# Routing's one-hot matrices with the tile index innermost in pairs, made and multiplied in two halves

## The reference

```
logits = xf @ router_w.T + router_b            # layer 0: 32 experts, the best one
idx = argmax(logits); h = relu(x @ W1[idx] + b1[idx]); out = relu(h @ W2[idx] + b2[idx])
probs = softmax(xf @ gate_w + gate_b)          # layer 1: 8 experts, the best two, weighted
out = sum over the best two of weight * (gelu(x @ W1[e] + b1[e]) @ W2[e] + b2[e])
values, idx = top_k(x @ Wg + bg + bias, 2)     # layer 2: 8 experts, the best two
out = sum over the best two of softmax(values) * (relu(x @ W1[e] + b1[e]) @ W2[e] + b2[e])
```

## Time and profile before

| | us |
|---|---|
| median of three runs | 2290.98 |
| profiled execution, its own time | 2291.57 |
| its span in the profile | 2289.7 |
| TensorE busy | 1947.9 (85%) |
| VectorE busy | 1574.2 (69%) |
| ScalarE busy | 1111.3 (49%) |
| GpSimd busy | 443.3 (19%) |

### The profile page before, as it was taken

One profiled execution on the slowest core, in us unless ns is written; L12 is line 12 of the kernel. 1 busy time (PEld: TensorE's weight loads), 2 busy tenths in 40 slices (PEclk: granted clock), 3 DMA queues, 4 the chain that ended last, 5 costly groups with the idle time before them and its releaser, 6 DMA issues.

```text
span 2289.7 us, 42272 instructions
## 1 busy us (share of the span) xinstructions
PE 1947.9 (85%) x15872; PEld 1314.7 (57%) x15872; DVE 1574.2 (69%) x3183; ACT 1111.3 (49%) x2198; POOL 443.3 (19%) x455
## 2 busy tenths in 40 slices
PE   6999296899999999749966698669967999999788
PEld 3877263688888887637744577557754222222343
DVE  6866665655555577746667888645567999999555
ACT  7555275523223244427745677346545223232654
POOL 0000474100000022137741000057620000000000
PEclk9999697999999999969987899879988999999899
DMA  6999367556566589556754567433332343232000
GB/s 197 315 343 328 122 151 163 210 199 246 219 230 243 220 324 404 191 191 218 231 165 133 148 168 179 164 98 93 85 110 73 115 122 90 82 90 85 0 21 29
DMA packets 236971, 389.10 MB, mean 170 GB/s; under 512 B 20640, under 2 KB 189216, under 8 KB 221025
## 3 DMA queue, kind: packets, MB, share of 16 engines
q1 hardware_dynamic: 211972, 333.86, 44.4%
q0 software_dynamic: 15296, 43.88, 7.3%
q10 hardware_dynamic: 9504, 8.65, 1.2%
HBM read 304.55 MB, written 81.78 MB: 169 GB/s over the span
## 4 chain that ended last, share of the span: by engine, by line
PE 51%; DVE 27%; ACT 8%; DMA 8%; issue 4%; POOL 2%; SPq 1%; ACTq 0%; DVEq 0%; POOLq 0%
DVE BIG L2819 7%; PE ps L1078 6%; PE ps L1080 6%; PE ps L1079 6%; PE ps L283 5%; PE ps L284 4%; PE ps L285 4%; PE ps L2320 4%; PE ps L2641 4%; DMA BIG<-in_adjT 3%; PE ps L2647 2%; PE ps L2322 2%; DMA X<-rows_split,idxg 2%; DVE BIG L1735 2%; DVE BIG L1743 2%
## 5 line engine op out<-in xcount | busy, mean ns | idle before, releaser
L1078 PE MATMUL ps<-R,BIG 128*128 128x256 f16 (+1 forms) x1764 | 486.1, 276 | 13.4 <-DVE BIG L1110 8.6
L1080 PE MATMUL ps<-R,BIG 128*128 128x256 f16 (+1 forms) x1764 | 483.5, 274 | 0.0
L1079 PE MATMUL ps<-R,BIG 128*128 128x256 f16 x1764 | 483.4, 274 | 0.0
L2641 PE MATMUL ps<-BIG 128*64 128x452 f32 x1056 | 230.9, 558 | 23.9 <-DVE BIG L2819 20.1
L1078 PEld LDWEIGHTS ps<-R,BIG 128*128 128x128 f16 x1764 | 171.9, 97 | 41.3 <-DVE BIG L1110 9.1
L2819 DVE SCALAR_TENSOR_TENSOR BIG<-BIG 128x904 f32<-128x904 f32 x176 | 192.4, 1155 | 1.6
L1079 PEld LDWEIGHTS ps<-R,BIG 128*128 128x128 f16 x1764 | 173.8, 98 | 21.5
L1080 PEld LDWEIGHTS ps<-R,BIG 128*128 128x128 f16 x1764 | 172.0, 98 | 24.5
L2703 ACT ACTIVATE BIG<-X,BIG 128x64 f32<-128x64 f32 x264 | 70.2, 337 | 232.8 <-PE ps L2647 232.7
L2641 PEld LDWEIGHTS ps<-BIG 128*64 128x64 f32 x1056 | 64.4, 136 | 186.4 <-issue 131.1
L2320 PE MATMUL ps<-BIG,X 128*128 x464 | 155.6, 382 | 9.6 <-DVE X L2379 9.6
(11 more groups left out here) (419 smaller groups left out, 4489.8 us busy)
## 6 DMA issues: line engine op xcount, KB each, us to landing
BIG<-adj_split SPq DMA_DIRECT2D x63, 1376.0 KB, 6.5
BIG<-in_adjT SPq DMA_DIRECT2D x42, 1408.0 KB, 10.8
BIG<-in_adj SPq DMA_DIRECT2D x22, 1408.0 KB, 9.2
BIG<-in_adjT SPq DMA_DIRECT2D x66, 452.0 KB, 3.3
adj_split<-BIG SPq DMA_DIRECT2D x21, 1376.0 KB, 10.9
XX<-in_f SPq DMA_DIRECT2D x70, 256.0 KB, 7.9
experts_split<-XX SPq DMA_DIRECT2D x64, 256.0 KB, 4.4
BIG<-experts_split SPq DMA_DIRECT2D x16, 1024.0 KB, 13.0
```

Source lines behind the costliest of these rows:

```text
L1078: pe.matmul(out[:, 0:n], pr[:, 0, k, :], h[:, k, 0:n], start=start, stop=False)
L1079: pe.matmul(out[:, 0:D], pr[:, 0, k, :], l[:, k, 0:D], start=False, stop=False)
L1080: return pe.matmul(out[:, 0:n], pr[:, 1, k, :], h[:, k, 0:n], start=False, stop=stop)
L2641: pe.matmul(ps[rs, 2 * (h // 2) + c, 0:CW], self.G[:, u, h * HF:(h + 1) * HF], self.PT[:, u, h, cs], start=start, stop=stop)
```

## The change

Four things change. The one-hots are laid out with the tiles of rows in pairs innermost: element (pair of tiles, lane or list tile, which of the two). The numbers 0 to 127 and 0 to J-1, each doubled, come from two small tables that GpSimd writes into X2 (`lanes`, `tiles`; semaphore `tb`) in each of the three layers. VectorE makes the one-hots choice by choice, in A parts (one in layer 0, two in layers 1 and 2), and raises `oh` after each; TensorE multiplies each part as it is ready and reads R and T with a step of two elements. ScalarE loads Gelu's table at the end of layer 1's routing. In the experts of layers 1 and 2 TensorE does hidden(0) ahead of turn(1).

```diff
-                s.wait(pe, "oh", 1)
                 J = self.J
-                n = self.A * KT
-                R, T = self.R(), self.T()
-                for q in range(n):
-                    mm = pe.matmul(ps[:, 0, 0:2 * J], R[:, q, :], T[:, q, :], start=q == 0, stop=q == n - 1)
+                for a in range(self.A):
+                    s.wait(pe, "oh", a + 1)
+                    R, T = self.R(a), self.T(a)
+                    for q in range(KT):
+                        mm = pe.matmul(ps[:, 0, 0:2 * J], R[:, q // 2, :, q % 2], T[:, q // 2, :, q % 2], start=a + q == 0,
+                                       stop=a == self.A - 1 and q == KT - 1)
                 mm.then_inc(s["lm"], 1)
...
+            def pairs(space, at, n, count=PR):
+                return space[:, at:at + n * count].bitcast(F16).rearrange("p (q c r) -> p q c r", q=count, r=2)
+
+            def R(self, a):
+                return self.pairs(XX, a * P * PR, P)
+
+            def T1(self, a):
+                return self.pairs(XX, P * KT + a * self.J * PR, self.J)
+
+            def T(self, a):
+                return self.pairs(X2, P * KT + a * self.J * KT, 2 * self.J)
+
+            def lanes(self):
+                return self.pairs(X2, 0, P, 1)
+
+            def tiles(self):
+                return self.pairs(X2, P, self.J, 1)
+
+            def tables(self, pool, *free):
+                for z, n in free:
+                    pool.wait_ge(z, n)
+                for out, row16, n in ((self.lanes(), lane16, P), (self.tiles(), tile16, self.J)):
+                    pool.tensor_copy(out, row16[:, 0:n].rearrange("p (q c o) -> p q c o", q=1, o=1).to_broadcast([P, 1, n, 2]))\
+                        .then_inc(self.st["tb"], 1)
...
                 W[self.i + 1].act(act)
+                if self.kind == "softmax":
+                    act.preload_act_table_set("gelu_and_others")
...
-                v.tensor_tensor(T1, tile16[:, 0:J].rearrange("p (o j) -> p o j", o=1).to_broadcast([P, q, J]),
-                                high.rearrange("p (q o) -> p q o", o=1).to_broadcast([P, q, J]), ALU.is_equal)
-                link(v.tensor_tensor(R, lane16[:, :].rearrange("p (o c) -> p o c", o=1).to_broadcast([P, q, P]),
-                                     low.rearrange("p (q o) -> p q o", o=1).to_broadcast([P, q, P]), ALU.is_equal))
-                v.tensor_scalar(T2[:, :, 0:J], T1, pos1[:, 0:1], None, ALU.mult)
-                v.tensor_tensor(T2[:, :, J:2 * J], T1, which[:, 0:q].rearrange("p (q o) -> p q o", o=1).to_broadcast([P, q, J]),
-                                ALU.mult).then_inc(s["oh"], 1)
+                s.wait(v, "tb", 2)
+                for a in range(A):
+                    T1, T2 = self.T1(a), self.T(a)
+
+                    def tile_row(z, n):
+                        return z[:, a * KT:(a + 1) * KT].rearrange("p (q o r) -> p q o r", o=1, r=2).to_broadcast([P, PR, n, 2])
+
+                    v.tensor_tensor(T1, self.tiles().to_broadcast([P, PR, J, 2]), tile_row(high, J), ALU.is_equal)
+                    link(v.tensor_tensor(self.R(a), self.lanes().to_broadcast([P, PR, P, 2]), tile_row(low, P), ALU.is_equal))
+                    v.tensor_scalar(T2[:, :, 0:J, :], T1, pos1[:, 0:1], None, ALU.mult)
+                    v.tensor_tensor(T2[:, :, J:2 * J, :], T1, tile_row(which, J), ALU.mult).then_inc(s["oh"], 1)
...
                 turn(0)
+                hidden(0)
                 turn(1)
-                hidden(0)
...
             p0.pool(pool)
+            r0.tables(pool, LC.done[1], s0.st.end("tx"))
             r0.pool(pool)
...
             p1.pool(pool)
+            r1.tables(pool, (p1.st["ag"], p1.st.at("ag") + 2 * KT + KT))
             many_rows.pool(pool)
...
             c1.pool(pool)
+            r2.tables(pool, *e1.done, *top.done)
             p2.pool(pool)
```

More of the change, by code:

```diff
@@ L1779, in __init__ @@
                 self.J, self.G, self.size = TILES[E], GROUPS[E], GROUP[E]
-                self.st = Stage("route", lm=1, v=0, a={"argmax": 0, "softmax": 2, "top2": 2}[kind], mk=1, rk=2, oh=1, ix=1,
-                                cw=1, sel=16 if i == 0 else 16 * 9)
+                self.st = Stage("route", lm=1, v=0, a={"argmax": 0, "softmax": 2, "top2": 2}[kind], mk=1, rk=2, oh=self.A, ix=1,
+                                cw=1, tb=2, sel=16 if i == 0 else 16 * 9)
                 self.done = [self.st.end("cw"), self.st.end("sel")]
@@ L1824, in pe @@
                 mm.then_inc(s["rk"], 1)
-                s.wait(pe, "oh", 1)
                 J = self.J
-                n = self.A * KT
-                R, T = self.R(), self.T()
-                for q in range(n):
-                    mm = pe.matmul(ps[:, 0, 0:2 * J], R[:, q, :], T[:, q, :], start=q == 0, stop=q == n - 1)
-                mm.then_inc(s["lm"], 1)
[L1833 to L1841, removed]
+                for a in range(self.A):
[4 more added lines that the diff above has]
+                                       stop=a == self.A - 1 and q == KT - 1)
+                mm.then_inc(s["lm"], 1)
+            @staticmethod
+            def pairs(space, at, n, count=PR):
[16 more added lines that the diff above has]
+                        .then_inc(self.st["tb"], 1)
             def act(self, act):
@@ L1953, in dve @@
                 link(v.tensor_copy(low, posu[:, 0:A, :].rearrange("p a t -> p (a t)")))
-                q = A * KT
-                R, T1, T2 = self.R(), self.T1(), self.T()
-                v.tensor_tensor(T1, tile16[:, 0:J].rearrange("p (o j) -> p o j", o=1).to_broadcast([P, q, J]),
-                                high.rearrange("p (q o) -> p q o", o=1).to_broadcast([P, q, J]), ALU.is_equal)
-                link(v.tensor_tensor(R, lane16[:, :].rearrange("p (o c) -> p o c", o=1).to_broadcast([P, q, P]),
-                                     low.rearrange("p (q o) -> p q o", o=1).to_broadcast([P, q, P]), ALU.is_equal))
-                v.tensor_scalar(T2[:, :, 0:J], T1, pos1[:, 0:1], None, ALU.mult)
-                v.tensor_tensor(T2[:, :, J:2 * J], T1, which[:, 0:q].rearrange("p (q o) -> p q o", o=1).to_broadcast([P, q, J]),
-                                ALU.mult).then_inc(s["oh"], 1)
+                s.wait(v, "tb", 2)
[7 more added lines that the diff above has]
+                    v.tensor_tensor(T2[:, :, J:2 * J, :], T1, tile_row(which, J), ALU.mult).then_inc(s["oh"], 1)
                 G = self.G
```

## The result

The changed kernel takes 2272.89 us (median of 4 runs, 2270.41 to 2274.25), the kernel before 2290.99 in the same comparison (4 runs, 2286.65 to 2292.18). The ratio is 0.9922, 95% interval [0.9906, 0.9937]: 18.1 us less, where 17.5 were forecast. The profiled execution took 2273.15 us, its span is 2271.3. Lines have moved: L1956, L1958, L1960, L1961, L1966 and L1982 of before are now L1981, L1982, L1983, L1984, L1988 and L2004; the indices' L1990 is L2012, the gathers' L2264 is L2286, turn's L2296 is L2318, ScalarE's copy L2343 is L2365.

What follows compares the result with a forecast made beforehand. In three routings VectorE's one-hots, then in layers 1 and 2 TensorE's matmuls, were taken as the bound. 2.65 + 7.3 + 6.75 (layers 0, 1, 2) + 0.8 (experts) = 17.5 us less, 2273.5 us; range 2266 to 2286.

Steps and rivals of the forecast that it cites:

- The rate: VectorE's one-hots in the routings: paired operands cost 0.52 ns an element instead of 1.04, bounds 0.26 and 1.04.
- rival A: VectorE's one-hots: pairs bring no rate, only overlap of halves gains; 3.7 us saved, 2287.3 us; 10%.
- E: VectorE's one-hots: rereading one pair costs each tick, 0.78 ns an element; 10.5 us saved, 2280.5 us; 5%.
- The lane product: VectorE's product L1960 in the routings: its rate stays at 0.26 ns an element, 0.46 us per half.
- TensorE's step of two: Routing matmuls reading operands with a two-element step: a pair stays at 0.10 us, at most 0.20.
- B: Routing matmuls: TensorE's step costs what f32 does, 0.20 us a pair; 13.5 us saved, 2277.5 us; 12%.
- C: Routing matmuls: TensorE becomes the bound; break-even at 0.31 us a pair, at 0.40 9.7 us slower, 2300.7 us; 5%.
- The halves: Layers 1 and 2 routing: first half's matmuls overlap VectorE's second; with the rate, L1982 starts 7.3 and 6.75 us sooner.
- The tables and the loads: GpSimd's table copies, 0.4 us each, and b2's rows ahead of the experts are covered by idle time: cost 0.
- The activation table: Gelu's table load moved ahead of layer 1's experts: worth 0, bounds 0 and 1.28 us.
- hidden(0) ahead of turn(1): TensorE's order in the experts: 0.8 us less in layer 2, bounds 0.25 lost and 1.4 gained; layer 1's cost covered.
- Rival D: Layer 1's experts: GpSimd's 7.22 us stand ends at its own moment, not with the gathers; 10.2 us saved, 2280.8; 6%.

Runs made afterwards that it cites:

- E2: Changed kernel with the old layout (tiles outermost, step of 0 innermost), one-hots still in halves; 2282.03 us, ratio 0.9973.
- E5: Changed kernel with T2 in two blocks, one per product, instead of side by side in each pair of tiles; 2272.95 us, ratio 0.9924.
- E4: Changed kernel without the early load of Gelu's table; 2273.01 us, ratio 0.9931.
- E9: Changed kernel plus one unread single-column GpSimd subtraction right behind the all-reduce; 2268.98 us, ratio 0.9903.
- E1: Changed kernel with pairs but one part for both choices: one signal, then all 44 matmuls; 2271.1 us, ratio 0.9922.
- E8: The kernel before the change, unedited, profiled a second time; 2290.05 us.
- E6: Changed kernel with layer 1's two GpSimd table copies behind the all-reduce instead of ahead of it; 2273.51 us, ratio 0.9924.
- E3: Changed kernel with TensorE's old order turn(0), turn(1), hidden(0) in the experts of layers 1 and 2; 2272.58 us, ratio 0.9925.
- E7: Changed kernel with both T2 in two blocks and layer 1's table copies behind the all-reduce; 2273.69 us, ratio 0.9918.

## Why the prediction was right

**The rate.** Forecast 0.52 ns an element between bounds of 0.26 and 1.04; it is 1.62 us for 2816 elements less some 0.15, so 0.52. E2 excludes rival A, and 1.62 instead of some 2.4 excludes E: at 0.52 ns an element, the pair that is read again and again costs nothing extra. The Trainium skill ("Vector Engine (DVE) Microarchitecture Reference", section 5.1) had this rate, and the trace agrees; its section 5.2, read as a price for words without a neighbour, would have given 0.86 ns, and the trace has nothing of it.

**The lane product.** This is the one term that the routings missed. The prediction said of L1960 that its "rate stays (0.26)". It went to 0.52 ns (0.79 us from start to start, less 0.14, for 1276), 0.33 us more per half, 0.66 in layers 1 and 2 and 0.3 in layer 0: 1.6 of the 16.7 us forecast for the routings, of which 15.1 came. The step priced the source's layout and forgot the destination's: 22 or 44 pieces with gaps became 11.

**TensorE's step of two.** Taken as free: a pair every 0.105 us, weight loads 142 ns. Rivals B and C (0.20 and over 0.31 us a pair) are out.

**The halves.** The first burst ends at 986.94, well ahead of the second half (988.41), so the second burst starts with that half and ends (990.85) just ahead of L2004 (990.96), together with VectorE's own tail. Both hang on the same instruction, L1984 of the second half: that is why E5's saving ahead of it came through in full up to L2004, 0.65 us a layer, and why the lane product's loss did too.

**The tables and the loads.** The table copies and b2's rows are hidden, as forecast: the two copies take 0.39 and 0.27 us (0.4 each was the estimate) and end 46 us ahead of the one-hots in layer 1. One load is missing from the prediction: that of the small weights, which doesn't move up with the indices. ScalarE rounds the last of them at 997.82 and then reads the experts' numbers, so layer 1's copy 0 starts at 1000.04, 0.50 us behind the end of turn(0) (999.54); in layer 2 it is 0.04. E4, without the table load, has 0.44, so the load of the table isn't the cause. In the changed kernel TensorE's 1.20 us ahead of turn(3) cover it.

**The activation table.** 0, as forecast (E4), with the stand in place.

**hidden(0) ahead of turn(1).** Forecast 0.8 us in layer 2, measured 0. The failing step is "with its 4.0 us": the 4.0 were taken from where the matmuls had stood, with the clock of 0.63 that the prediction gives for them; moved up, they ran at 0.52 and took 4.9. The bound of 5.0 us at 0.5 had been worked out and was the better value: ahead of turn(0) TensorE had stood 5.81 us, and the granted clock was still low while the moved matmuls ran.

**Rival D.** Refuted in the form that it had: the stand moved up with the gathers. E9 shows what it is, and that it costs some 2 us in layer 1 of the changed kernel.

**The sum.** Forecast 17.5, measured 18.1. The routings gave 1.6 less and the order 0.8 less than forecast, so what the runs support by mechanism is 15.1 to 15.4 us. The other 3 us come from no step of the change that any run shows, and that they made up for the two misses is luck. The ratio's interval is 14.4 to 21.5 us and holds both numbers. The forecast hit the time more closely than its steps deserved.

## What to carry to other kernels

Look for an innermost step of 0 (one element repeated) of two-tensor f16 instructions: where the repeat can be moved out by one place, so that every operand has two neighbours innermost, the time halves (3.08 to 1.62 us), and TensorE reads the interleaved matrices at no cost. When a layout changes, price the destination as well as the sources, and count its pieces: 11 with gaps cost 0.33 us that one block does not, and 22 kept the full rate. Take a matmul's price from the place where it will stand, with the clock of that place; and where GpSimd mixes an all-reduce with ordinary work, put a cheap ordinary instruction of the later kind behind the all-reduce, in idle time.

## What the runs showed that was not expected

- GpSimd stands 7.2 to 8.4 us (the changed kernel, E1 to E8) ahead of its first TENSOR_TENSOR behind a partition all-reduce, from a pair of MODIFY_POOL_CONFIG on, even if that comes 34 us and six gathers later; copies (0.46 and 0.34 us) and gathers run without it (E6), and one TENSOR_TENSOR of a single column takes it (11.78 us, E9). The Trainium skill ("GPSIMD Engine Reference", section 2.1) has about 6 us for the first call of freshly loaded code; here it is the way back to ordinary instructions that shows, at 7.2 to 8.4; that code is loaded in it no row shows.
- A TENSOR_SCALAR in f16 ran at 0.26 ns an element into one block or 22 pieces and at 0.52 into 11 pieces with gaps (E1, E5).
- From layer 0's first experts to layer 1's one-hots the kernel before took 694.3 and 695.1 us in two executions, and the changed kernel 696.1, where E1, E3, E5 and E7, with hardly another instruction in that stretch, had 693.3, 698.5, 694.4 and 695.4. An edit worth under 2 us is to be judged by its own stage and not by the span.
